# Four transformer blocks on one core: shorter prologues, and the division by the sums on VectorE tile by tile

## The chip, the core and the metric

The kernel runs on one core of a Trainium2 chip. Its engines work from queues of their own: TensorE (PE, with its weight loads as PEld), VectorE (DVE), ScalarE (ACT), GpSimd (POOL) and SyncE (SP, which issues the transfers here). The metric is the device time of one execution in microseconds (us); less is better.

## The reference

The input x is 4 x 1024 x 512 in float32. Four blocks are added to it, each on a layer norm of what the one before left:

```python
x = x + squared_attention(layernorm(x))   # 16 heads of 32; weights (q.k)**2, causal; o / (z + EPS); Wo
x = x + gated_attention(layernorm(x))     # a gate picks one key and one value head per token; causal softmax
x = x + multi_query_attention(layernorm(x))  # one key and value head, biases, causal softmax, output product
x = x + gated_attention(layernorm(x))
```

In each attention, the weights of a query are summed over its keys, the products of weights and values are divided by that sum, and the result goes through an output product or (gated) a plain transposition.

## The kernel before

The program has two acts. The first holds the squared attention, one stage for each of the 4 batch items. The second holds 12 softmax stages: gated, multi-query, gated, 4 items each. A stage has 4 phases of 4 heads. A phase has 20 halves: in each even half PE scores a burst of keys (`keys`, 10 a phase: keys on partitions, up to 512 queries beside), whose exponentials ACT writes to one of 5 slots of `probs`; in 9 of the odd halves PE scores a burst of the next phase's queries (`rows`), of which DVE takes the maxima (L961, L966) that the next phase's exponentials need. Bursts go through three pairs of PSUM banks, two pairs a burst, so that PE can't fill the second pair of a key burst before DVE has read the first pair of the row burst ahead of it. GpSimd masks the diagonal tiles (`keys`, L758) and adds the probabilities up over the key tiles (`add`, L774 to L781), into `added`. PE multiplies probabilities and values (`av`, parts A and B for the first and second chunk of 512 queries, C for the rest of the second) into `y`, and sums `added` over partitions (`sm`); ACT copies the sums to `sums`. DVE inverts them in place, four tiles of 128 columns for each chunk (`inv`, L1068), and GpSimd multiplies the 512 columns of `y` by the inverses (`nrm`, L829). The last chunk of all does both on DVE (`last_nrm`, L1062, L1063).

All else (the next stage's norm, queries, keys, values, gates and the outputs `out` of the stage before) is work that fills PE between the bursts. It goes through two further PSUM banks, cut in pieces, and each bank is free again when ACT or DVE has emptied it: for `kall` and `vall` (all heads' keys and values of a tile, of which the gate picks one) by a multiplication and a reduction on DVE (L945, L949). Python makes one list of events, and each engine runs its own part of that list in its order. `phase` places the fixed events in the halves; `spread` gives each half filling work in proportion to a table of room, which `phase` raises by `INVERTED` in a half with an inverse. Each act begins with a prologue: what its first phase needs, written out ahead of the first half by `plan` and `keys_and_values`. In the first act these are values (`v2`), queries and keys (`q2`, `k2`) and the keys' variances (`ksq` and `kvar`, whose powers GpSimd takes, L821), for two phases.

Of the kernel before, what the change touches and what calls it, by code (L numbers as in the profile page):

```python
# [90 lines left out]
INVERTED = 0.85  # L91

# [27 lines left out]
def keys_and_values(kind, s):  # L120

    if kind == "squared":
        values = [("v2", s, pair, n) for pair in range(2) for n in range(NT // 2)]
        between = values[0:2] + values[4:6]
        return between, values[2:4] + values[6:8] + features(4 * s), features(4 * s + 1)
    queries = [[("q", 4 * s + g, c) for c in range(NC)] for g in range(2)]
    if kind == "gated":
        first = [("gt", s, 1), ("gtt", s, 0), queries[0][0], ("gtt", s, 1), ("gate", s), ("gate_exp", s), queries[0][1], ("gate_value", s)]
        first += [("kall", s, t) for t in range(NT)]
        first.insert(len(first) - 1, ("krep", s, 0))  # L130
        first += [queries[1][0], ("krep", s, 1), ("kt", s, 0), queries[1][1], ("kt", s, 1)]
        return [("gt", s, 0)], first, [("vall", s, t) for t in range(NT)]
    rest = [("vs", s, 0), ("vs", s, 1), queries[1][0], ("vst", s, 0), queries[1][1], ("vst", s, 1)]
    return [("ks", s, 0), queries[0][0]], [("ks", s, 1), queries[0][1]], rest
# [33 lines left out]
def sums_done(kind, ph, c):  # L168

    if kind != "squared":  # L170

        return [(("inv", ph, c, n), min(n + 1, 3 + c)) for n in range(TPC)] + [(("nrm", ph, c), 3 + c)]
    return [(("nrm", ph, c), 2)]


def phase(kinds, ph):
# [34 lines left out]
    for c in range(NC):  # L211
        of = ph - c
        if of < 0:
            continue
        first = SUMS_AT[c] - (4 if final and c == 0 else 0)
        at[first].append(("sm", of, c))
        for event, later in sums_done(kinds[of // NG], of, c):
            at[first + later].append(event)
            if event[0] == "inv":
                room[first + later] += INVERTED  # L220
# [3 lines left out]
def since(event):  # L224

    event = event[1] if event[0] == "more" else event
    if event[0] in ("q", "q2", "k2"):
# [96 lines left out]
def plan(kinds):  # L324
# [7 lines left out]
    else:  # L332
# [5 lines left out]
        events += between + first  # L338
    if soft:
        rows = [("rows", 0, k) for k in range(NRB)]  # L340
        for n in range(max(len(rows), len(rest))):
# [6 lines left out]
    else:  # L348
        events += rest
    for s in range(stages):  # L350
# [33 lines left out]
        else:  # L384
            own = [[("q", 4 * s + g, c) for c in range(NC)] for g in (2, 3)]
            work = [(head[0], 1), (sprinkled(parted(own[0]), head[1]), HALVES - 2), (mixed(parted(outs[:half]), parted(own[1]), kinds), 2 * HALVES - 2)]
        if s == stages - 1:
# [26 lines left out]
class Signals:  # L414


    def __init__(self, nc, ctx):
# [34 lines left out]
        self.inverted = sem("inverted")  # L452
# [117 lines left out]
def act_program(nc, sg, k, psum, m, weights, stages, source, result, dram):  # L570
# [91 lines left out]
    with nc.Block() as block:  # L662
# [61 lines left out]
        def _(pool):  # L724
# [17 lines left out]
            for e in events:  # L742
# [81 lines left out]
                elif u == "nrm" and soft:  # L824
                    _, ph, c = e
                    pool.wait_ge(sg.inverted, place["inv", ph, c, TPC - 1] + 1)
                    wait_free(pool, ("av", ph, "AC"[c]))
                    out = y_of(ph)[:, CHUNK * c:CHUNK * c + CHUNK]
                    pool.tensor_tensor(out, out, m["sums"][:, c], ALU.mult).then_inc(sg.normalized, 1)  # L829
# [8 lines left out]
        def _(act):  # L838
# [19 lines left out]
            for e in events:  # L858
# [57 lines left out]
                elif u == "sm":  # L916
                    _, ph, c = e
                    if ph:
                        act.wait_ge(sg.normalized, place["nrm", ph - 1, c] + 1)
# [3 lines left out]
        def _(dve):  # L923
# [27 lines left out]
            for e in events:  # L951
# [112 lines left out]
                elif u == "inv":  # L1064
                    _, ph, c, n = e
                    wait_free(dve, ("sm", ph, c))
                    some = tile_of(m["sums"][:, c], n)
                    dve.reciprocal(some, some).then_inc(sg.inverted, 1)  # L1068
# [19 lines left out]
        def _(pe):  # L1088
# [55 lines left out]
            for event in events:  # L1144
# [168 lines left out]
                elif u == "out":  # L1313
                    _, s, t = e
                    out = free(e)
                    for g in range(NG):
                        ph = NG * s + g
                        if ("nrm", ph, t // TPC) in place:
                            pe.wait_ge(sg.normalized, place["nrm", ph, t // TPC] + 1)
# [75 lines left out]
```

## Time and profile before

| | us |
|---|---|
| median of 3 runs | 4017.52 (4014.93 to 4022.45) |
| profiled execution, device time | 4020.66 |
| its span, from first to last instruction | 4018.9 |
| PE busy | 3647.1 (91%) |
| GpSimd busy | 2982.7 (74%) |
| DVE busy | 2170.1 (54%) |
| ACT busy | 1624.3 (40%) |

A busy share is an average over stages with different limits. Idle time of an engine counts only where another one waits for it. PE's records overlap and their ends are modelled, so its busy time is read as an occupancy, and its idle time (span less busy) as what waits cost it. The first act ends near 1011 us, the second runs to the end.

### The profile page before, as it was taken

The numbers are of one execution on the slowest core, as the hardware profiler recorded it, in microseconds if no ns is written. First come the engines' busy times: TensorE is split into PE (matmuls) and PEld (weight loads), VectorE is DVE, ScalarE is ACT, GpSimd is POOL, SyncE is SP. The second block draws the span as 40 slices with busy tenths as digits, with TensorE's granted clock in tenths as the row PEclk, the third lists the DMA queues.
The fourth block names the chain that finished last, engine by engine and source line by source line (L and its number), as shares of the span: only waits on it lengthen the run. The fifth ranks groups of instructions, "written<-read, shape, count | busy, mean of one in ns | idle before, by whom it ended". The sixth has DMA issues, their size and how long they took to land.

```text
span 4018.9 us, 66697 instructions
## 1 busy us (share of the span) xinstructions
PE 3647.1 (91%) x25570; PEld 1450.4 (36%) x25570; DVE 2170.1 (54%) x5132; ACT 1624.3 (40%) x2433; POOL 2982.7 (74%) x2207
## 2 busy tenths in 40 slices
PE   8899999997989999999888888888998999999976
PEld 5343534432333333333333333333333333333332
DVE  1222323233556766666666656565665666676663
ACT  1554545554043333434444434343332334343343
POOL 3988788896067767777888877787667677776786
PEclk9999999998999999999999999999999999999997
DMA  2000101020110010100101010010101001010011
GB/s 74 27 6 27 38 16 48 6 70 33 45 33 1 32 32 1 64 1 25 40 13 53 6 48 12 30 35 17 48 1 35 30 1 64 1 54 1 1 43 32
DMA packets 63286, 115.02 MB, mean 29 GB/s; under 512 B 8576, under 2 KB 9088, under 8 KB 62976
## 3 DMA queue, kind: packets, MB, share of 16 engines
q1 hardware_dynamic: 62976, 110.75, 8.5%
q8 instruction: 211, 3.46, 0.4%
q14 instruction: 99, 0.81, 0.1%
HBM read 77.17 MB, written 33.55 MB: 28 GB/s over the span
## 4 chain that ended last, share of the span: by engine, by line
PE 54%; DVE 7%; ACT 6%; issue 4%; POOL 3%; DMA 0%; POOLq 0%; SPq 0%; DVEq 0%; ACTq 0%
PE banks L1181 11%; PE banks L1134 11%; PE banks L1166 9%; PE banks L1228 8%; PE banks L1127 7%; ACT probs_soft L870 5%; PE banks L1163 3%; DVE banks L966 3%; PE banks L1327 3%; DVE maxima_soft L961 2%; POOL added_soft L781 2%; PE banks L1195 1%; DVE rest_soft L1085 1%; DVE maxima_soft L966 1%; PE banks L1325 0%
## 5 line engine op out<-in xcount | busy, mean ns | idle before, releaser
L870 ACT ACTIVATE probs_soft<-banks 128x1024 f32<-128x1024 f32 (+1 forms) x960 | 848.4, 936 | 1195.1 <-PE banks L1166 1171.2
L781 POOL TENSOR_TENSOR added_soft<-added_soft,probs_soft 128x512 f32<-128x512 f32 (+1 forms) x380 | 1153.0, 3034 | 21.3 <-POOL added_soft L774 6.4
L966 DVE CUSTOM_DVE_ANT_0 banks<-banks,mask 128x128 f32<-128x128 f32 (+3 forms) x1536 | 701.3, 528 | 516.5 <-PE banks L1181 516.0
L961 DVE TENSOR_REDUCE maxima_soft<-banks 128x2 f32<-128x1024 f32 x384 | 452.6, 1221 | 367.5 <-PE banks L1181 367.4
L1181 PE MATMUL banks<-k_soft,q_soft 32*128 32x512 f32 (+3 forms) x4608 | 499.7, 525 | 77.6 <-ACT probs_soft L870 77.4
L876 ACT ACTIVATE probs_squared<-banks,key_scale_squared 128x512 f32<-128x512 f32 (+3 forms) x768 | 379.7, 590 | 341.5 <-PE banks L1166 337.1
L1127 PE MATMUL banks<-xnT,wide 128*128 128x512 f32 x1024 | 509.9, 620 | 5.0 <-DVE rest_soft L1085 1.9
L1134 PE MATMUL banks<-wide,xnT 128*128 128x512 f32 x1024 | 497.0, 613 | 1.0 <-ACT q_soft L853 1.0
L1166 PE MATMUL banks<-q_soft,k_soft 32*128 32x512 f32 (+3 forms) x4608 | 476.0, 495 | 0.0
L758 POOL TENSOR_SCALAR_AFFINE_SELECT probs_soft<-probs_soft 128x512 f32<-128x512 f32 x384 | 239.4, 637 | 313.8 <-ACT probs_soft L870 308.3
L1228 PE MATMUL banks<-probs_soft,v_soft 128*32 128x512 f32 (+3 forms) x4608 | 438.3, 499 | 20.2 <-ACT q_soft L855 4.8
L774 POOL TENSOR_TENSOR added_soft<-probs_soft 128x2048 f32<-128x2048 f32 x48 | 216.7, 4514 | 270.9 <-ACT probs_soft L870 270.9
L781 POOL TENSOR_TENSOR added_squared<-added_squared,probs_squared 128x512 f32<-128x512 f32 (+1 forms) x124 | 378.3, 3051 | 4.5 <-POOL added_squared L774 1.4
L1068 DVE RECIPROCAL sums_soft<-sums_soft 128x128 f32<-128x128 f32 x380 | 338.1, 924 | 16.7 <-ACT sums_soft L853 16.6
L1181 PEld LDWEIGHTS banks<-k_soft,q_soft 32*128 32x128 f32 x4608 | 184.1, 186 | 358.5 <-issue 353.4
L1163 PE MATMUL banks<-shift_soft,ones 32*128 32x512 bf16 (+3 forms) x2304 | 197.9, 332 | 88.1 <-DVE maxima_soft L966 57.6
L1134 PEld LDWEIGHTS banks<-wide,xnT 128*128 128x128 f32 x1024 | 175.9, 189 | 262.9 <-issue 251.1
L1127 PEld LDWEIGHTS banks<-xnT,wide 128*128 128x128 f32 x1024 | 178.3, 192 | 254.2 <-issue 236.2
L1228 PEld LDWEIGHTS banks<-probs_soft,v_soft 128*32 128x32 f32 x4608 | 122.3, 110 | 329.7 <-issue 225.1
L1166 PEld LDWEIGHTS banks<-q_soft,k_soft 32*128 32x128 f32 x4608 | 213.2, 187 | 24.4 <-issue 20.9
L966 DVE DVE_READ_ACCUMULATOR2_ANT maxima_soft<- 128x1 f32 x1536 | 220.6, 144 | 0.0
L1163 PEld LDWEIGHTS banks<-shift_soft,ones 32*128 32x128 bf16 x2304 | 62.9, 91 | 417.3 <-issue 390.3
(136 smaller groups left out, 4075.7 us busy)
## 6 DMA issues: line engine op xcount, KB each, us to landing
tiles<-out SPq DMA_DIRECT2D x96, 256.0 KB, 2.7
rest_soft<-out SPq DMA_DIRECT2D x96, 256.0 KB, 2.9
out<-rest_soft SPq DMA_DIRECT2D x96, 256.0 KB, 2.1
tiles<-in_x SPq DMA_DIRECT2D x32, 256.0 KB, 2.7
rest_squared<-in_x SPq DMA_DIRECT2D x32, 256.0 KB, 2.8
out<-rest_squared SPq DMA_DIRECT2D x32, 256.0 KB, 2.0
wide<-in_gated_wqkvT SPq DMA_DIRECT2D x3, 1024.0 KB, 7.6
probs_squared<-in_squared_wk SPq DMA_DIRECT2D x1, 1024.0 KB, 5.5
```

The source lines that it names most:

```text
L781: ins = pool.tensor_tensor(sums, sums, slot(ph, n)[:, :, col:col + width], ALU.add)
L870: ins = act.activation(slot(ph, n)[:, 2 * a:2 * a + 2, 0:width], score_pair(e, a)[:, :, 0:width], ACT.Exp, scale=SCALE)
L876: ins = act.activation(slot(ph, n)[:, i, col:col + cols], score_pair(e, a)[:, x, col:col + cols], ACT.Square, scale=m["key_scale"][:, ph % ...
L961: ins = dve.reduce_max(m["maxima"][:, ph % 2, 2 * a:2 * a + 2, t, p], score_pair(e, a)[:, :, col:col + width], AX_X)
L966: ins = dve.tensor_tensor_reduce(scores, scores, k["mask"][:, CHUNK - width:CHUNK], 1.0, MASKED, ALU.add, ALU.max, m["maxima"][:, ph % 2, ...
L1068: dve.reciprocal(some, some).then_inc(sg.inverted, 1)
L1127: ins = pe.matmul(out, wt[:, kc, cols], m["xnT"][:, kc, CHUNK * c:CHUNK * c + CHUNK], start=(kc == 0), stop=(kc == KC - 1))
L1134: ins = pe.matmul(out, m["xnT"][:, kc, P * t:P * t + P], wt[:, kc, cols], start=(kc == 0), stop=(kc == KC - 1))
L1163: pe.matmul(psum[:, score_bank(e, i), col:col + width], k["ones16"][D * i:D * i + D, :], m["shift"][D * i:D * i + D, ph % 2, c, q0:q0 + wi ...
L1166: ins = pe.matmul(psum[:, score_bank(e, i), col:col + width], k_of(ph)[D * i:D * i + D, P * kb:P * kb + P], m["q"][D * i:D * i + D, ph % N ...
L1181: ins = pe.matmul(psum[:, score_bank(e, i), col:col + P * blocks], m["q"][D * i:D * i + D, ph % NG, P * t:P * t + P], k_of(ph)[D * i:D * i ...
L1228: ins = pe.matmul(out[D * i:D * i + D, q0:q0 + width], left, slot(ph, n)[:, i, col:col + width], start=(x == 0), stop=(x == len(products) ...
```

## The change

Four things are changed. In the first act the prologue keeps half of the values and the features of one phase; the other half and the features of the second phase become filling work of the first phases. In the second act's prologue one query product and two value tiles move behind the first row burst or into the first phase. `INVERTED` goes, so that halves with an inverse get no more filling work than others. And the softmax stages' `nrm` on GpSimd goes: DVE multiplies each tile of 128 columns right behind its inverse, each product with a wait for the inverse ahead of it. `out` then waits for single tiles.

```diff
-INVERTED = 0.85
@@ keys_and_values
+        if s == 0:
+            return [("gt", s, 0)], first + [("krep", s, 1), queries[1][0], ("kt", s, 0), ("kt", s, 1)], \
+                [queries[1][1]] + [("vall", s, t) for t in range(NT)]
         first += [queries[1][0], ("krep", s, 1), ("kt", s, 0), queries[1][1], ("kt", s, 1)]
@@ sums_done
-        return [(("inv", ph, c, n), min(n + 1, 3 + c)) for n in range(TPC)] + [(("nrm", ph, c), 3 + c)]
+        return [(("inv", ph, c, n), min(n + 1, 3 + c)) for n in range(TPC)]
@@ phase
             at[first + later].append(event)
-            if event[0] == "inv":
-                room[first + later] += INVERTED
@@ since
+    if event[0] == "v2" and event[1] == 0 or event[0] in ("q2", "k2") and event[1] < NG:
+        return 0
@@ plan
-        events += between + first
+        values = [e for e in between + first if e[0] == "v2"]
+        events += [e for e in values if e[2] == 0] + [e for e in first if e[0] != "v2"]
+        behind_first = [(in_pieces(rest, kinds), HALVES - 2), (in_pieces([e for e in values if e[2]], kinds), 2 * HALVES + 4)]
     if soft:
         rows = [("rows", 0, k) for k in range(NRB)]
+        behind_first = [(in_pieces(rest[len(rows) - 2:], kinds), 6)]
+        rest = rest[:len(rows) - 2]
...
-    else:
-        events += rest
...
+        if s == 0:
+            work = work[:1] + behind_first + work[1:]
@@ gpsimd
-                elif u == "nrm" and soft:
-                    _, ph, c = e
-                    pool.wait_ge(sg.inverted, place["inv", ph, c, TPC - 1] + 1)
-                    wait_free(pool, ("av", ph, "AC"[c]))
-                    out = y_of(ph)[:, CHUNK * c:CHUNK * c + CHUNK]
-                    pool.tensor_tensor(out, out, m["sums"][:, c], ALU.mult).then_inc(sg.normalized, 1)
@@ scalar, sm
-                        act.wait_ge(sg.normalized, place["nrm", ph - 1, c] + 1)
+                        act.wait_ge(sg.normalized, place[("inv", ph - 1, c, TPC - 1) if soft else ("nrm", ph - 1, c)] + 1)
@@ vector, inv
                     wait_free(dve, ("sm", ph, c))
-                    some = tile_of(m["sums"][:, c], n)
-                    dve.reciprocal(some, some).then_inc(sg.inverted, 1)
+                    wait_free(dve, ("av", ph, "AC"[c]))
+                    some, out = tile_of(m["sums"][:, c], n), tile_of(y_of(ph)[:, CHUNK * c:CHUNK * c + CHUNK], n)
+                    then(dve.reciprocal(some, some))
+                    dve.tensor_tensor(out, out, some, ALU.mult).then_inc(sg.normalized, 1)
@@ tensor, out
-                        if ("nrm", ph, t // TPC) in place:
-                            pe.wait_ge(sg.normalized, place["nrm", ph, t // TPC] + 1)
+                        done = ("inv", ph, t // TPC, t % TPC) if soft else ("nrm", ph, t // TPC)
+                        if done in place:
+                            pe.wait_ge(sg.normalized, place[done] + 1)
```

DVE, in the second multi-query stage, from the end of the last row burst of a phase (L966) to the first row burst behind it, before:

```order
L966 ISA banks,maxima_soft<-banks,mask 128x512
L966 ISA maxima_soft 128x1
L974 TENSOR_REDUCE minus_max_soft<-maxima_soft 128x4x4
L1068 RECIPROCAL sums_soft<-sums_soft 128x128 x4
L966 ISA banks,maxima_soft<-banks,mask 128x128
```

And after:

```order
L964 ISA banks,maxima_soft<-banks,mask 128x512
L964 ISA maxima_soft 128x1
L972 TENSOR_REDUCE minus_max_soft<-maxima_soft 128x4x4
L1067 RECIPROCAL sums_soft<-sums_soft 128x128
L1068 TENSOR_TENSOR y_soft<-y_soft,sums_soft 128x128
L1067 RECIPROCAL sums_soft<-sums_soft 128x128
L1068 TENSOR_TENSOR y_soft<-y_soft,sums_soft 128x128
L1067 RECIPROCAL sums_soft<-sums_soft 128x128
L1068 TENSOR_TENSOR y_soft<-y_soft,sums_soft 128x128
L1067 RECIPROCAL sums_soft<-sums_soft 128x128
L1068 TENSOR_TENSOR y_soft<-y_soft,sums_soft 128x128
L964 ISA banks,maxima_soft<-banks,mask 128x128
```

Between the two row bursts stand four inverses and four products in turn, where four inverses stood.

GpSimd, in the same phase, from the first addition of its second chunk (L774; L778 after) to the mask of the next phase's first key burst, before:

```order
L774 TENSOR_TENSOR added_soft<-probs_soft 128x2048
L781 TENSOR_TENSOR added_soft<-added_soft,probs_soft 128x2048
L758 AFFINE_SELECT probs_soft<-probs_soft 128x4x128
L829 TENSOR_TENSOR y_soft<-y_soft,sums_soft 128x512
L781 TENSOR_TENSOR added_soft<-added_soft,probs_soft 128x2048
L758 AFFINE_SELECT probs_soft<-probs_soft 128x4x128 x2
L781 TENSOR_TENSOR added_soft<-added_soft,probs_soft 128x2048
L758 AFFINE_SELECT probs_soft<-probs_soft 128x4x128
L781 TENSOR_TENSOR added_soft<-added_soft,probs_soft 128x4x384
L781 TENSOR_TENSOR added_soft<-added_soft,probs_soft 128x4x128
L829 TENSOR_TENSOR y_soft<-y_soft,sums_soft 128x512
L758 AFFINE_SELECT probs_soft<-probs_soft 128x4x128
```

And after:

```order
L778 TENSOR_TENSOR added_soft<-probs_soft 128x2048
L785 TENSOR_TENSOR added_soft<-added_soft,probs_soft 128x2048
L762 AFFINE_SELECT probs_soft<-probs_soft 128x4x128
L785 TENSOR_TENSOR added_soft<-added_soft,probs_soft 128x2048
L762 AFFINE_SELECT probs_soft<-probs_soft 128x4x128 x2
L785 TENSOR_TENSOR added_soft<-added_soft,probs_soft 128x2048
L762 AFFINE_SELECT probs_soft<-probs_soft 128x4x128
L785 TENSOR_TENSOR added_soft<-added_soft,probs_soft 128x4x384
L785 TENSOR_TENSOR added_soft<-added_soft,probs_soft 128x4x128
L762 AFFINE_SELECT probs_soft<-probs_soft 128x4x128
```

The two divisions of `y` are gone, and masks and additions stand in the order in which they stood.

PE, from the first act's values (L1288) on, before (L1127 are queries and keys, L1296 variances, L1166 scores of keys):

```order
L1288 MATMUL banks<-wide,xnT 128x256 x64
L1127 MATMUL banks<-xnT,wide 128x512 x16
L1296 MATMUL banks<-head_mean,key_square_squared 128x4 x8
L1127 MATMUL banks<-xnT,wide 128x512 x16
L1296 MATMUL banks<-head_mean,key_square_squared 128x4 x8
L1166 MATMUL banks<-q_squared,k_squared 128x512 x4
L1127 MATMUL banks<-xnT,wide 128x512 x4
L1166 MATMUL banks<-q_squared,k_squared 128x384 x4
```

And after:

```order
L1288 MATMUL banks<-wide,xnT 128x256 x32
L1127 MATMUL banks<-xnT,wide 128x512 x16
L1296 MATMUL banks<-head_mean,key_square_squared 128x4 x8
L1166 MATMUL banks<-q_squared,k_squared 128x512 x4
L1127 MATMUL banks<-xnT,wide 128x512 x6
L1166 MATMUL banks<-q_squared,k_squared 128x384 x4
L1166 MATMUL banks<-q_squared,k_squared 128x128 x4
L1127 MATMUL banks<-xnT,wide 128x512 x6
```

Ahead of the first scores, 32 products of values, 16 of queries and keys and 8 of variances are gone; they follow between the scores.

## Rows read from the trace of the kernel before

**Rows 1.** stretches: us, busy PE, PEld, DVE, ACT, POOL (instructions), PEclk, DMA

```profile
96.00:256.30 160.30, 139.06 (x861) 67.86 (x862) 48.10 (x54) 87.27 (x173) 144.26 (x87) 0.94 0.06 21
...
1598.00:1846.00 248.00, 234.32 (x1729) 88.68 (x1729) 164.82 (x416) 95.01 (x126) 180.30 (x143) 0.99 0.08 27
2057.30:2269.30 212.00, 184.82 (x1609) 69.56 (x1610) 141.86 (x375) 96.49 (x125) 179.48 (x142) 0.98 0.10 31
```

**Rows 2.** PE's waits from 2057.3 to 2269.3 us, multi-query stage

```profile
PE banks L1163 <- DVE maxima_soft L966: 10.2, 15, 1.6
```

**Rows 3.** groups of instructions, whole program: busy us, mean ns, idle before

```profile
L781 POOL TENSOR_TENSOR added_soft<-added_soft,probs_soft 128x512 f32<-128x512 f32 (+1 forms) x380 | 1153.0, 3034 | 21.3 <-POOL added_soft L774 6.4 <-POOL shift_cols_soft L794 0.2 <-POOL added_soft L781 0.2
...
L1068 DVE RECIPROCAL sums_soft<-sums_soft 128x128 f32<-128x128 f32 x380 | 338.1, 924 | 16.7 <-ACT sums_soft L853 16.6
...
L829 POOL TENSOR_TENSOR y_soft<-y_soft,sums_soft 128x512 f32<-128x512 f32 x95 | 121.0, 1274 | 0.0
```

**Rows 4.** the divisions of DVE by line: duration ns min/median/max

```profile
L1063 DVE TENSOR_TENSOR y_soft<-y_soft,sums_soft x4: 291/291/291, 4008.6 to 4012.1; 128x128 f32<-128x128 f32 x4
...
L1076 DVE TENSOR_TENSOR y_squared<-y_squared,sums_squared x31: 691/2323/4984, 140.6 to 968.5; 128x512 f32<-128x512 f32 x31
```

**Rows 5.** GpSimd and DVE at 467 us (start us, us, engine, line)

```profile
467.41 4.51 POOL L781 TENSOR_TENSOR added_squared<-added_squared,probs_squared 128x2048 f32<-128x2048 f32 x1 [0.17 <-POOL added_squared L774]
...
467.50 4.98 DVE L1076 TENSOR_TENSOR y_squared<-y_squared,sums_squared 128x512 f32<-128x512 f32 x1
```

**Rows 6.** GpSimd and DVE at 1189 us

```profile
1189.55 1.27 POOL L781 TENSOR_TENSOR added_soft<-added_soft,probs_soft 128x512 f32<-128x512 f32 x1
1189.60 1.37 DVE L1010 TENSOR_TENSOR gate_soft<-chosen_soft,top_soft 128x128 f32<-128x128 f32 x1
```

**Rows 7.** timeline, end of a phase in the multi-query stage

```profile
2211.96 4.54 POOL L781 TENSOR_TENSOR added_soft<-added_soft,probs_soft 128x2048 f32<-128x2048 f32 x1
...
2213.65 3.38 DVE L1068 RECIPROCAL sums_soft<-sums_soft 128x128 f32<-128x128 f32 x4
...
2217.04 4.79 POOL L781 TENSOR_TENSOR added_soft<-added_soft,probs_soft 128x1536 f32<-128x1536 f32 x2
...
2219.66 0.30 DVE L966 CUSTOM_DVE_ANT_0 banks<-banks,mask 128x128 f32<-128x128 f32 x1 [2.63 <-PE banks L1181]
...
2221.45 0.34 PE L1163 MATMUL banks<-shift_soft,ones 32*128 32x384 bf16 x4 [0.17 <-DVE maxima_soft L966]
```

**Rows 8.** timeline, middle of the same phase

```profile
2196.43 1.75 DVE L1068 RECIPROCAL sums_soft<-sums_soft 128x128 f32<-128x128 f32 x2
...
2197.59 4.52 POOL L781 TENSOR_TENSOR added_soft<-added_soft,probs_soft 128x2048 f32<-128x2048 f32 x1 [0.17 <-POOL added_soft L774]
...
2199.69 2.36 DVE L961 TENSOR_REDUCE maxima_soft<-banks 128x2 f32<-128x1024 f32 x2 [1.51 <-PE banks L1181]
...
2201.06 0.40 PE L1163 MATMUL banks<-shift_soft,ones 32*128 32x512 bf16 x4 [0.15 <-DVE maxima_soft L961]
```

**Rows 9.** timeline, end of a phase in a gated stage

```profile
1530.96 3.38 DVE L1068 RECIPROCAL sums_soft<-sums_soft 128x128 f32<-128x128 f32 x4
...
1534.36 4.77 POOL L781 TENSOR_TENSOR added_soft<-added_soft,probs_soft 128x1536 f32<-128x1536 f32 x2
...
1540.53 1.71 PE L1228 MATMUL banks<-probs_soft,v_soft 128*32 128x512 f32 x16
```

**Rows 10.** timeline of PE, first act: prologue, and a unit of values later

```profile
79.03 13.98 PE L1127 MATMUL banks<-xnT,wide 128*128 128x512 f32 x32
...
163.60 3.72 PE L1288 MATMUL banks<-wide,xnT 128*128 128x256 f32 x16
```

**Rows 11.** timeline of PE, end of the second act's prologue

```profile
1097.75 3.70 PE L1134 MATMUL banks<-wide,xnT 128*128 128x512 f32 x8
```

**Rows 12.** timeline, last phase of all

```profile
3980.66 5.01 DVE L1068 RECIPROCAL sums_soft<-sums_soft 128x128 f32<-128x128 f32 x6 [1.05 <-ACT sums_soft L853]
...
3993.36 3.71 PE L1325 MATMUL banks<-ident,y_soft 128*128 128x128 f32 x16 [7.91 <-POOL y_soft L829]
```

More of the change, by code:

```diff
@@ L451, in __init__ @@
         self.last_normalized = sem("last_normalized")
-        self.inverted = sem("inverted")
         self.normalized = sem("normalized")
```

## The prediction

> **What bounds the kernel now.** I read the table of engines first, then stretches, the waits in them, the groups of instructions, and at last the timeline around the inverses. PE is busy 91% of the span and the other engines 40 to 74%, so PE's order of work is the bound, and a gain has to come out of PE's idle time. The stretches tell where that is [rows 1]: the first phases after the prologue leave PE 160.30 − 139.06 = 21.2 us idle, a gated stage 248.00 − 234.32 = 13.7 us (3.4 a phase) and a multi-query stage 212.00 − 184.82 = 27.2 us (6.8 a phase), at granted clocks of 0.94, 0.99 and 0.98, so nearly all at the 2.4 GHz level. In the multi-query stage GpSimd is busy 85% (179.48) and DVE 67% (141.86); of PE's waits there one is for DVE's maxima: 15 times, 10.2 us in all, 1.6 at the longest [rows 2]. DVE is off the bound on average, but once or more a phase PE stands at a pair of banks that DVE has yet to read. What the change adds to DVE is therefore priced at those places and not as a share of busy time.
>
> **The division by the sums.** GpSimd loses 95 products of 512 columns, 121.0 us; DVE gets 380 of 128 columns, one behind each of 380 inverses of 924 ns [rows 3]. Alone, a product of this shape takes DVE 291 ns (the last chunk's four, when GpSimd has nothing to do) [rows 4]. So 380 × 0.29 = 110 us of DVE work replace 121.0 of GpSimd's, if nothing else acts.
>
> Something else acts. The same division in the first act, 512 columns, takes 691 ns at the least, 2323 in the middle and 4984 at most [rows 4]. Its longest starts 0.09 us behind a GpSimd addition of 4.51 us and ends at 472.48, which is 0.56 us behind the addition's end at 471.92 [rows 5]. A 128x128 product of the second act starts 0.05 us behind an addition of 1.27 us, takes 1.37 instead of some 0.29, and ends 0.15 behind the addition [rows 6]. So a DVE product with both inputs in SBUF is held until the GpSimd operation under way is done. The inverses, one input each, aren't held: four take 3.38 us beside an addition of 4.54 [rows 7], and the mean of all is 924 ns.
>
> A rule of the Trainium skill speaks to this ("SBUF — State Buffer", section Who interferes with whom): a VectorE instruction with two SBUF inputs contends with a GpSimd instruction that reads SBUF, over a port pair that whoever issues first locks, and the other is fully blocked. The 4984 ns of rows 5 and the 1370 ns of rows 6 agree with it. By that rule the change sends 380 instructions into the lock; without it they would be 0.29 us each.
>
> Each held product also holds up the inverse behind it. I walk the three places that recur, putting each product at the end of the addition that it meets.
>
> End of a multi-query phase [rows 7]. The inverses start at 2213.65. The first ends at 2214.5; its product is held to the end of the addition, 2211.96 + 4.54 = 2216.5, or 2216.1 if GpSimd is 0.35 earlier for the missing division (my allowance). The second inverse ends 0.9 later, inside the next two additions (4.79 us together), and since one follows the other without a gap its product is out at the end of the first (1.27 and 3.45 by the order's shapes, the longer ahead), near 2220.3. The last two pairs are out near 2221.7 and 2222.9. DVE is free at about 2223.0, where it was at 2213.65 + 3.38 = 2217.03: 6.0 us later. It waited 2.63 us for PE there and read the next row burst from 2219.66; it now reads it from 2223.0, 3.3 us late, and the key burst whose second pair PE filled at 2221.45, 0.17 behind DVE's maxima, follows as late. PE pays +3.3 us.
>
> Middle of the phase [rows 8]. Of two inverses from 2196.43 the first product is out by 2197.6, the second meets the addition of 2197.59 to 2202.11 and is out at 2202.3. DVE turned to the row burst at 2199.69 with 1.51 us of slack; it is 2.6 late, and PE, 0.15 behind it at 2201.06, loses about +2.4. The two first inverses of a chunk stand in a half of their own, and I allow 0.5 for theirs: 6.2 a phase where there is little filling work.
>
> End of a gated phase [rows 9]. The inverses end at 1534.34; with the products, two of them held by the 4.77 us of additions, at about 1539.5, 5.2 later. DVE's reading of key products for the gate comes behind it and frees the bank of `av` part C (1540.53) 2 to 3 us later; PE has filling work for part of that. I take 2 us, and 1.5 for the middle: 3.5 a phase.
>
> About 19 phases are light (multi-query ones and the last ones) and 27 full: 19 × 6.2 + 27 × 3.5 = 118 + 95 = 213 us. PE's idle time a phase is already 6.8 and 3.4 us [rows 1], as large as these stalls, and a stall that falls before another wait shortens it. I take a third off: +142. Ends: 40, if lateness mostly falls into the idle time that there is (with the gains below that is 4025), and 260, if each stall adds up and the halves with more products pay too. Below nothing it can't go: nothing that PE waits for gets earlier by more than GpSimd's relief. That relief is small: `out` already stands a phase behind its division, and the adds start 0.35 us to 1.3 earlier in a queue of GpSimd that seldom ends last; −2 (0 to −20).
>
> **The first act's prologue.** Four units of values of 3.72 us and the second phase's features, 13.98 [rows 10], go behind the first scores: 14.9 + 14.0 = 28.9 us of PE work. It isn't saved; it fills. The three phases from 96 us have 21.2 us idle [rows 1], of which some 3.4 a phase are left in a well-filled stage, so about 11 can be filled; and some work ran while the clock was lower (0.94 against 0.99 later), worth 0.05 × 160 = 8 at most, half taken. −15, from −5 (the moved values come with waits for DVE's copies, and for GpSimd's powers of the variances) to −27 (all but the 1.9 that doesn't fit).
>
> **The second act's prologue.** Two units of value tiles, 3.70 each [rows 11], and a query product move behind the first row burst. PE then waits there for maxima and exponentials that start earlier: −3, from −5 to +1.
>
> **Room without `INVERTED`.** The filling work of a stage stays as it was; the last halves of a phase get less and the early ones more. The early halves have part of the 3.4 and 6.8 us idle, the late ones get shorter just where DVE is now late (counted above). Over 48 phases I take 0.2 each: −10, from −25 to +10.
>
> **The end.** PE's 7.91 us wait for GpSimd's last division goes, but the six inverses ahead of it, from 3980.66 [rows 12], now carry products beside GpSimd's last additions: 0, from −8 to +3.
>
> Sum: 142 − 2 − 15 − 3 − 10 = +112. On the profiled execution's 4020.66 us (span 4018.9) that is 4133; the median of the runs is 3.1 lower, so 4130. The case's own range, from the stalls' two ends with the other terms, is 4025 to 4240.
>
> **Rivals.**
> *The cover holds, and it is faster.* The products slip between GpSimd's operations, or DVE's lateness at the next row burst stays under the slack that it has (2.63 and 1.51 us in rows 7 and 8); it decides as long as a cluster of inverses ends less than about 2 us later than before. For it: DVE is idle 46% of the span, and L781's additions fill only 1153 of the second act's some 3000 us [rows 3]. Against: the inverses stand in the order just where additions follow each other without a gap. Then −15 − 3 − 10 − 5 = −33: 3985.
>
> The Trainium skill speaks for this rival ("GPSIMD Engine Reference", section 4.1 Engine selection): elementwise work belongs on VectorE, GpSimd being about twice as slow with two inputs. Rows 3 and 4 agree, 1274 ns against 4 × 291, but these four ran while GpSimd was idle.
>
> *DVE becomes the bound.* L781's additions fill 1153 of the second act's some 3000 us; a product that starts at any moment would be held 0.38 × 3034 / 2 = 0.6 us, and behind long additions, as in the walks, more: I take 1.1. 380 × 1.1 + 110 = 530 us more on DVE, and where PE follows DVE burst by burst three quarters of it, 400, show: 4390. For it: rows 2 and 7, where PE starts 0.17 us behind DVE. Against: DVE would still have 2170 + 530 = 2700 of 4100 us.
>
> *The gains and the stalls cancel.* Half of the lower end of the stalls, 30, against 30: within some 8 us of 4017, if only the ends of multi-query phases are hit.
>
> **How the numbers follow.** Slower by held products 0.68; the cover holds 0.20; DVE the bound 0.06; cancelling 0.06, of which 0.04 lie within 0.2% (8 us, about what a measurement of this kernel can tell from no change) and 0.01 to each side. Faster 0.21, same 0.04, slower 0.75. The likeliest case gives 4130. The range takes in the rival on the other side, 3985, and reaches to the upper end of the likeliest case, 4240; DVE as the bound is left out.
>
> **What would show it.** The group of `y_soft` products on DVE with a mean of 1.2 to 1.6 us (0.29 proves the holding wrong); DVE's busy time near 2600 to 2700; more and longer waits of PE for `maxima_soft` in the multi-query stages, 3 us where 1.6 was the longest; the GpSimd group of 95 divisions gone, and its additions no longer than 3034 ns. The first act should end some 15 us earlier whatever the second does. If the products are held and PE's waits for maxima don't grow, the cover was larger than rows 7 and 8 say; if the first act isn't shorter, the moved work met waits for DVE.

## The result and the profile after

The changed kernel takes 4317.05 us (4315.86 to 4318.33, four runs) where the kernel before took 4018.23 beside it: a ratio of 1.0743, 95% interval 1.0724 to 1.0762. The forecast was slower by 112 us, with 4240 as the upper end; it is 299 us, and outside the range. Direction and place were as forecast; the size was not.

Stretches of the changed kernel, in the columns of [rows 1]: the three phases that were 96 to 256.3 us, the gated stage, the multi-query stage, and then what lies ahead of the second act's first burst of keys and what lies behind it. PEclk is the share of TensorE's clock that was granted: 1.00 is 2.4 GHz, 0.50 is 1.2.

```profile
69.30:239.30 170.00, 164.66 (x965) 84.48 (x964) 49.89 (x62) 90.22 (x176) 148.10 (x89) 0.98 0.07 19
1633.00:1908.20 275.20, 243.66 (x1729) 89.64 (x1730) 200.03 (x448) 95.01 (x125) 171.08 (x135) 0.96 0.07 24
2162.90:2413.10 250.20, 197.74 (x1609) 73.55 (x1609) 182.14 (x408) 95.92 (x124) 170.45 (x134) 0.92 0.08 26
0.00:1088.60 1088.60, 999.21 (x5475) 454.87 (x5476) 332.56 (x457) 489.43 (x956) 811.11 (x507) 0.97 0.11 36
1088.60:4315.70 3227.10, 2746.01 (x20096) 1011.77 (x20096) 2287.73 (x5056) 1135.36 (x1478) 2065.78 (x1605) 0.95 0.07 23
```

The kernel before, its second act from the first burst of keys on:

```profile
1105.70:4018.90 2913.20, 2643.62 (x20080) 990.69 (x20080) 1833.27 (x4672) 1135.87 (x1478) 2172.28 (x1700) 0.98 0.08 26
```

The second act's first burst of keys comes 17.1 us earlier (1088.6, was 1105.7), and of the 21.2 us idle of the first act's first phases 170.00 − 164.66 = 5.3 are left. Not all of the 17.1 is the first act's. PE's first product of the second act, after and before:

```profile
1005.85 1.92 PE L1140 MATMUL banks<-xnT,g_wg 128*32 128x512 f32 x16 [3.97 <-PEq L1331]
...
1015.89 2.64 PE L1140 MATMUL banks<-xnT,g_wg 128*32 128x512 f32 x16 [3.99 <-PEq L1330]
```

So the first act gains 10.0 us, and the other 7.1 are the second act's shorter prologue, whose moved work is done later. From the first burst of keys on (called the second act from here) the kernel is 313.9 us longer. PE's idle time in it went from 2913.20 − 2643.62 = 269.6 to 3227.10 − 2746.01 = 481.1, +211.5; the other 102.4 us are PE's own busy time, for as many matmuls (20096, 20080), at a granted clock of 0.95 where it was 0.98.

Groups of the changed kernel, against [rows 3]:

```profile
L785 POOL TENSOR_TENSOR added_soft<-added_soft,probs_soft 128x512 f32<-128x512 f32 (+1 forms) x380 | 1152.9, 3034 | 20.9 <-POOL added_soft L778 5.9 <-ACT probs_soft L868 0.2 <-POOL added_soft L785 0.2
...
L1068 DVE TENSOR_TENSOR y_soft<-y_soft,sums_soft 128x128 f32<-128x128 f32 x380 | 447.3, 1177 | 13.0
...
L1067 DVE RECIPROCAL sums_soft<-sums_soft 128x128 f32<-128x128 f32 x380 | 357.7, 941 | 12.3 <-ACT sums_soft L851 12.2
```

A product takes 1177 ns in the mean in place of the 291 of [rows 4]: 447.3 − 380 × 0.291 = 337 us of holding. It is spread unevenly: half of the products take 442 ns or less, the longest 4616. The mean of GpSimd's additions is the same as before, 3034 ns: what waits is DVE. PE's largest waits in the whole run:

```profile
PE banks L1163 <- DVE maxima_soft L959: 105.7, 69, 5.5
PE banks L1163 <- DVE maxima_soft L964: 97.4, 57, 5.3
PE banks L1228 <- DVE picking_soft L943: 57.7, 21, 3.9
PE banks L1181 <- ACT probs_soft L868: 49.7, 107, 1.3
```

Before they read, for the same four:

```profile
PE banks L1181 <- ACT probs_soft L870: 77.4, 187, 1.4
PE banks L1163 <- DVE maxima_soft L966: 57.6, 70, 1.9
...
PE banks L1163 <- DVE maxima_soft L961: 22.4, 42, 1.4
...
PE banks L1228 <- DVE picking_soft L945: 4.7, 9, 0.5
```

Waits for maxima went from 80.0 to 203.1 us, those of `av` (L1228) for a bank in which DVE has yet to read the gate's keys and values (`picking_soft`) from 4.7 to 57.7, while those for ACT's exponentials fell by only 27.7.

The timeline of the changed kernel, middle of the phase that [rows 8] show:

```profile
2330.41 4.52 POOL L785 TENSOR_TENSOR added_soft<-added_soft,probs_soft 128x2048 f32<-128x2048 f32 x1 [0.17 <-POOL added_soft L778]
2331.42 3.67 DVE L1068 TENSOR_TENSOR y_soft<-y_soft,sums_soft 128x128 f32<-128x128 f32 x1
...
2335.01 2.34 DVE L959 TENSOR_REDUCE maxima_soft<-banks 128x2 f32<-128x1024 f32 x2
...
2336.36 0.40 PE L1163 MATMUL banks<-shift_soft,ones 32*128 32x512 bf16 x4 [3.01 <-DVE maxima_soft L959]
```

The second product starts 1.01 us into the addition and ends 0.16 behind it; DVE turns to the row burst at once, and PE, which was 0.15 behind DVE here, waits 3.01. The end of the same phase, where [rows 7] had four inverses in 3.38 us and PE 0.17 behind the maxima:

```profile
2346.98 4.51 POOL L785 TENSOR_TENSOR added_soft<-added_soft,probs_soft 128x2048 f32<-128x2048 f32 x1
...
2348.95 0.94 DVE L1067 RECIPROCAL sums_soft<-sums_soft 128x128 f32<-128x128 f32 x1
2349.93 1.71 DVE L1068 TENSOR_TENSOR y_soft<-y_soft,sums_soft 128x128 f32<-128x128 f32 x1
...
2352.10 4.79 POOL L785 TENSOR_TENSOR added_soft<-added_soft,probs_soft 128x1536 f32<-128x1536 f32 x2
2352.53 3.17 DVE L1068 TENSOR_TENSOR y_soft<-y_soft,sums_soft 128x128 f32<-128x128 f32 x1
...
2356.59 0.44 DVE L1068 TENSOR_TENSOR y_soft<-y_soft,sums_soft 128x128 f32<-128x128 f32 x1
...
2357.93 0.29 DVE L1068 TENSOR_TENSOR y_soft<-y_soft,sums_soft 128x128 f32<-128x128 f32 x1
2358.14 0.29 DVE L964 CUSTOM_DVE_ANT_0 banks<-banks,mask 128x128 f32<-128x128 f32 x1
...
2359.91 0.51 PE L1163 MATMUL banks<-shift_soft,ones 32*128 32x384 bf16 x4 [4.34 <-DVE maxima_soft L964]
...
2360.18 1.52 PE L1166 MATMUL banks<-q_soft,k_soft 32*128 32x384 f32 x8
```

Four inverses and products fill 2348.95 to 2358.22, 9.3 us. And the last row shows what came after the wait: eight matmuls of 384 columns in 1.52 us. Eighteen microseconds earlier they took

```profile
2342.50 0.81 PE L1166 MATMUL banks<-q_soft,k_soft 32*128 32x384 f32 x8
```

The granted clock in between (columns of [rows 1]):

```profile
2338.00:2344.00 6.00, 6.00 (x68) 1.93 (x64) 4.01 (x6) 2.49 (x4) 4.26 (x2) 1.00 0.00 0
2352.00:2358.90 6.90, 3.34 (x34) 0.98 (x32) 6.80 (x11) 1.55 (x2) 6.53 (x9) 1.00 0.00 1
2359.00:2365.70 6.70, 5.79 (x48) 2.54 (x48) 2.98 (x13) 1.94 (x2) 3.57 (x3) 0.50 0.00 0
2366.00:2372.00 6.00, 5.40 (x46) 2.49 (x49) 5.09 (x18) 2.26 (x4) 2.62 (x3) 1.00 0.00 0
```

PE is busy for 3.34 of the 6.90 us in which it waits for DVE, and then runs 6.7 us at 1.2 GHz (0.50). So this wait costs twice. Added up from the trace's records of the granted clock, the second act spends 335 us at 1.2 GHz, where it was 111; half of the 224 us between them, 112, is an estimate of what that costs, close to the 102 that PE's busy time grew.

### The profile page after: what moved, and what is told of

Read it like the earlier page. It is cut to its first block and busy times, and to the rows that moved or that the text cites. A ratio compares the mean times of both kernels' runs of the same rounds, so it can differ in the third digit from the quotient of the medians.

```text
span 4315.7 us, 67265 instructions
## 1 busy us (share of the span) xinstructions
PE 3745.2 (87%) x25570; PEld 1466.6 (34%) x25570; DVE 2620.3 (61%) x5512; ACT 1624.8 (38%) x2433; POOL 2876.9 (67%) x2112
## 5 line engine op out<-in xcount | busy, mean ns | idle before, releaser
L785 POOL TENSOR_TENSOR added_soft<-added_soft,probs_soft 128x512 f32<-128x512 f32 (+1 forms) x380 | 1152.9, 3034 | 20.9 <-POOL added_soft L778 5.9
L1181 PE MATMUL banks<-k_soft,q_soft 32*128 32x512 f32 (+3 forms) x4608 | 504.5, 529 | 51.5 <-ACT probs_soft L868 49.7
L1228 PE MATMUL banks<-probs_soft,v_soft 128*32 128x512 f32 (+3 forms) x4608 | 473.4, 533 | 66.5 <-DVE picking_soft L943 57.7
L1127 PE MATMUL banks<-xnT,wide 128*128 128x512 f32 x1024 | 514.6, 623 | 6.6 <-DVE rest_soft L1085 2.4
L1134 PE MATMUL banks<-wide,xnT 128*128 128x512 f32 x1024 | 508.4, 622 | 13.0 <-DVE picking_soft L943 12.8
L1166 PE MATMUL banks<-q_soft,k_soft 32*128 32x512 f32 (+3 forms) x4608 | 506.5, 523 | 0.0
L1068 DVE TENSOR_TENSOR y_soft<-y_soft,sums_soft 128x128 f32<-128x128 f32 x380 | 447.3, 1177 | 13.0
L778 POOL TENSOR_TENSOR added_soft<-probs_soft 128x2048 f32<-128x2048 f32 x48 | 216.7, 4514 | 340.5 <-ACT probs_soft L868 276.7
L1067 DVE RECIPROCAL sums_soft<-sums_soft 128x128 f32<-128x128 f32 x380 | 357.7, 941 | 12.3 <-ACT sums_soft L851 12.2
L1127 PEld LDWEIGHTS banks<-xnT,wide 128*128 128x128 f32 x1024 | 177.8, 192 | 260.2 <-issue 240.6
L1228 PEld LDWEIGHTS banks<-probs_soft,v_soft 128*32 128x32 f32 x4608 | 127.6, 115 | 406.6 <-issue 264.8
L1166 PEld LDWEIGHTS banks<-q_soft,k_soft 32*128 32x128 f32 x4608 | 225.8, 198 | 29.0 <-issue 24.3
```

Of the source, the lines that this page charges most:

```text
L785: ins = pool.tensor_tensor(sums, sums, slot(ph, n)[:, :, col:col + width], ALU.add)
L1067: then(dve.reciprocal(some, some))
L1068: dve.tensor_tensor(out, out, some, ALU.mult).then_inc(sg.normalized, 1)
L1127: ins = pe.matmul(out, wt[:, kc, cols], m["xnT"][:, kc, CHUNK * c:CHUNK * c + CHUNK], start=(kc == 0), stop=(kc == KC - 1))
L1134: ins = pe.matmul(out, m["xnT"][:, kc, P * t:P * t + P], wt[:, kc, cols], start=(kc == 0), stop=(kc == KC - 1))
L1166: ins = pe.matmul(psum[:, score_bank(e, i), col:col + width], k_of(ph)[D * i:D * i + D, P * kb:P * kb + P], m["q"][D * i:D * i + D, ph % N ...
```

## The experiments

Two theories stood against the held products (H in the expectations) at first: that the early halves, which take the filling work once INVERTED is gone, cost the time (R), and that a product on DVE costs by its work and waits, whatever GpSimd does (W).

**Products back on GpSimd.** The edit puts `nrm` back and takes the products out of `inv`; all else as changed:

```diff
-        return [(("inv", ph, c, n), min(n + 1, 3 + c)) for n in range(TPC)]
+        return [(("inv", ph, c, n), min(n + 1, 3 + c)) for n in range(TPC)] + [(("nrm", ph, c), 3 + c)]
...
-                    then(dve.reciprocal(some, some))
-                    dve.tensor_tensor(out, out, some, ALU.mult).then_inc(sg.normalized, 1)
+                    dve.reciprocal(some, some).then_inc(sg.inverted, 1)
```

> The changed kernel with the softmax stages' products back on GpSimd (512 columns at a time) and all else as changed. Theory H (products that are held behind GpSimd's additions make DVE late, PE waits for DVE, and its granted clock falls): the whole loss goes and the shorter prologues stay, 3985 to 4005 us, DVE busy near 2170. Rival R (taking INVERTED out put too much filling work into the early halves, and that is what costs): still over 4050 us.

3959.99 us, ratio to the kernel before 0.9849 (0.9834 to 0.9864): 357 us less than the changed kernel, and 25 under the lower end of what H gave. The products are the loss; R falls, and the other edits gain 61 us.

**Products alone**, on the kernel before (the same edit the other way round).

> The kernel before with only the products moved to DVE, tile by tile behind each inverse; prologues and INVERTED as before. Theory H: nearly the whole second act's loss of 314 us shows, 4300 to 4350 us, products with a mean near 1.2 us. Rival R: with the room behind inverses kept, the loss is under 230 us, below 4250.

4298.06 us, 1.0688 (1.067 to 1.0706): +277, 2 us under what H gave and far over R's 4250. Its products have a mean of 1252 ns. The two stages of [rows 1] in this run, where the room behind inverses is as before:

```profile
1635.80:1902.40 266.60, 237.59 (x1729) 90.57 (x1729) 207.56 (x448) 95.18 (x126) 171.06 (x135) 0.97 0.08 25
2147.30:2393.00 245.70, 194.12 (x1609) 72.23 (x1609) 181.22 (x407) 96.46 (x124) 169.88 (x133) 0.94 0.08 27
```

and PE's waits for ACT's exponentials in the whole run, 77.4 us before:

```profile
PE banks L1176 <- ACT probs_soft L863: 73.6, 180, 1.4
```

**Additions that only write.** The edit for one addition; the first ones of each chunk are replaced likewise:

```diff
+            def written(cells):
+                then(pool.memset(cells, 1.0))
+                then(pool.memset(cells, 1.0))
+                return pool.memset(cells[:, 0:HG // 2], 1.0)
...
-                        ins = pool.tensor_tensor(sums, sums, slot(ph, n)[:, :, col:col + width], ALU.add)
+                        ins = written(sums) if soft else pool.tensor_tensor(sums, sums, slot(ph, n)[:, :, col:col + width], ALU.add)
```

> The changed kernel in which GpSimd's additions of the softmax stages are replaced by fills of the same tiles (two and a half fills for each addition, so about as long: 4.6 us where an addition takes 4.5); the sums of the weights are left out by that. GpSimd then writes SBUF and reads none of it. Theory H: the products take 0.29 us, PE's waits for DVE's maxima fall from 203 us to about 80, and the time is 3980 to 4040 us. Rival W (the products are DVE work with waits of their own, and DVE is late by its amount of work, whatever GpSimd does): products stay near 1.2 us, the time over 4250.

3967.51 us, 0.9867 (0.9852 to 0.9881), 12 us under the range of H; the waits for maxima are 44.4 + 31.0 = 75.4 us. The fills keep GpSimd busy 615.8 + 615.8 + 331.3 = 1563 us, as long as the additions they replace (1152.9 + 216.7 + 164.8 = 1534). The end of a multi-query phase in this run, products now at L1073:

```profile
2147.33 1.80 POOL L748 MEMSET added_soft<- 128x2048 f32 x1
...
2148.17 0.29 DVE L1073 TENSOR_TENSOR y_soft<-y_soft,sums_soft 128x128 f32<-128x128 f32 x1
...
2149.36 0.29 DVE L1073 TENSOR_TENSOR y_soft<-y_soft,sums_soft 128x128 f32<-128x128 f32 x1
...
2153.83 0.34 PE L1168 MATMUL banks<-shift_soft,ones 32*128 32x384 bf16 x4 [0.17 <-DVE maxima_soft L969]
```

and the group of all products:

```profile
L1073 DVE TENSOR_TENSOR y_soft<-y_soft,sums_soft 128x128 f32<-128x128 f32 x380 | 120.2, 316 | 13.0
```

A product beside a GpSimd operation that reads no SBUF takes 0.29 us, and PE is back at 0.17 behind the maxima. W falls. The rule of the Trainium skill named in the prediction ("SBUF — State Buffer", Who interferes with whom) says the same: it is GpSimd's reading that contends, not its writing. Not held, the products are still no gain here: 3968 against 3960 on GpSimd, with intervals that touch, and with fills that run 29 us longer than the additions.

**The four products behind the last inverse**, in a row.

```diff
                     then(dve.reciprocal(some, some))
-                    dve.tensor_tensor(out, out, some, ALU.mult).then_inc(sg.normalized, 1)
+                    if n == TPC - 1:
+                        for n in range(TPC):
+                            some, out = tile_of(m["sums"][:, c], n), tile_of(y_of(ph)[:, CHUNK * c:CHUNK * c + CHUNK], n)
+                            dve.tensor_tensor(out, out, some, ALU.mult).then_inc(sg.normalized, 1)
...
-                        done = ("inv", ph, t // TPC, t % TPC) if soft else ("nrm", ph, t // TPC)
+                        done = ("inv", ph, t // TPC, TPC - 1) if soft else ("nrm", ph, t // TPC)
```

> The changed kernel with the four products of a chunk behind its fourth inverse, one after the other, and `out` waiting for all four. Theory H: one hold a chunk, at most one addition, and the other three products slip through behind it: the sum of the products falls from 447 us to 200 to 300, the time to 4130 to 4220 us. Rival W: same work of DVE, same time within 20 us of 4317. Rival H2 (each product is held anew, by the next addition, even when it is ready): the sum of the products rises over 600 us and the time over 4350.

4163.85 us, 1.0355 (1.0339 to 1.037); products 281.1 us, mean 799 ns. The holding fell from 337 to 281 − 111 = 170 us, and the loss against products on GpSimd from 357 to 204. H's figures hold, W's and H2's don't. The order of DVE's own instructions decides how long it is held.

**Each inverse a second time**, an edit of the run with products on GpSimd.

```diff
-                    dve.reciprocal(some, some).then_inc(sg.inverted, 1)
+                    then(dve.reciprocal(some, some))
+                    dve.reciprocal(some, some).then_inc(sg.inverted, 1)
```

> The changed kernel with its products on GpSimd (3960 us), and each inverse taken a second time in place, so that the sums themselves and not their inverses go into the products: DVE gets 380 operations of 0.94 us more, which nothing holds, where the held products took 1.18. Theory H (what costs is that DVE comes late to the next row burst, by whatever makes it late, and PE's granted clock then falls after its waits): 4130 to 4260 us, PE's waits for maxima over 140 us, and the time at the lower clock in the second act over 200 us where it was 89. Rival W (work that is not held is absorbed by DVE's idle time, only the hold itself costs): under 4000 us.

4120.73 us, 1.0251 (1.0236 to 1.0266): 161 more than the run with products on GpSimd, by 380 further inverses, 362 us of DVE work that nothing holds. That is 9 us under what H gave, and its 186 us at 1.2 GHz are under the 200; this experiment's W (such work is absorbed) is far off. PE's waits for maxima:

```profile
PE banks L1169 <- DVE maxima_soft L971: 71.4, 56, 3.5
...
PE banks L1169 <- DVE maxima_soft L966: 53.7, 58, 3.0
```

125 us where the expectation had over 140. So lateness of DVE behind the inverses costs by itself; holding is one way to make it late, and here a dearer one: 362 us of unheld work cost 161, 447 us of products with their holding 357. That it is dearer because it comes in lumps of up to 4 us wasn't tested.

**The gains apart**, each alone on the kernel before:

```diff
+    if event[0] == "v2" and event[1] == 0 or event[0] in ("q2", "k2") and event[1] < NG:
+        return 0
```

(with the first act's lines of `plan` from the change)

> The kernel before with only the first act's prologue shortened. By the trace of the changed kernel, whose first act ends 17 us earlier: 4001 to 4007 us where the kernel before has about 4021 on the same chip. Rival (what is moved only changes places, and the first act's end is set elsewhere): within 4 us of before.

4005.29 us, 0.9963 (0.9949 to 0.9977): −15. The expectation took all of the 17 us for the first act's. Over all the runs, the second act's first product starts at 999 to 1011 us with this prologue (nine profiles) and at 1016 to 1019 without it (four).

```diff
+        behind_first = [(in_pieces(rest[len(rows) - 2:], kinds), 6)]
+        rest = rest[:len(rows) - 2]
```

(with the lines of `keys_and_values` from the change)

> The kernel before with only the second act's prologue shortened. By the prediction, 3 us less; if a large part of the 61 us that the change gains without its products comes from here, 10 to 25 us less.

4024.23 us, 1.0009 (1.0000 to 1.0019): no gain, and 4 us lost at the edge of what can be told.

```diff
-INVERTED = 0.85
...
-            if event[0] == "inv":
-                room[first + later] += INVERTED
```

> The kernel before with only INVERTED taken out, the products on GpSimd. The change without its products gains 61 us, of which the first act has 18; if the rest is due to INVERTED, this one is 35 to 45 us faster than before. By the prediction, 10 us. Rival: no difference, the rest comes from the second prologue.

3965.74 us, 0.9866 (0.9851 to 0.988): −54, more than any of the figures expected. The second act, in the columns of [rows 1]:

```profile
1107.40:3962.80 2855.40, 2630.57 (x20083) 980.73 (x20080) 1836.92 (x4672) 1135.15 (x1478) 2170.18 (x1700) 0.99 0.08 27
```

Idle time is 224.8 where it was 269.6, and PE's busy time is 13 less. The waits for exponentials, 77.4 before, are

```profile
PE banks L1177 <- ACT probs_soft L866: 58.0, 123, 1.3
```

**INVERTED back in the changed kernel.**

```diff
+INVERTED = 0.85
...
+            if event[0] == "inv":
+                room[first + later] += INVERTED
```

> The changed kernel with INVERTED put back. The products alone cost 277 us on the kernel before, and the prologues together with INVERTED's removal 19 us more, though without the products they give 61. Theory I (the extra filling work behind inverses is PE's cover where DVE is late: its removal gains 54 us without held products and costs some 30 with them): 4275 to 4300 us, faster than the changed kernel's 4317. Rival A (the edits add up: INVERTED's removal gains here too): 4340 to 4380 us.

4284.36 us, 1.0659 (1.0641 to 1.0677): 33 us faster than the changed kernel, in the range of theory I and well under A's. The same edit that gains 54 us where products run on GpSimd costs 33 where they are held. From this run to the changed kernel the waits of `av` for `picking_soft` go from 29.5 to 57.7 us and those for maxima from 178.3 to 203.1, while those for exponentials fall from 71.7 to 49.7. That fits I's reason, that the filling work behind inverses covers DVE's lateness; no run tests the reason apart. The single effects add up to the whole: 4018 − 15 + 4 + 277 + 33 = 4317.

**What gained by itself, together**: the first prologue and no INVERTED, products on GpSimd and the second prologue as before.

> The kernel before with the first act's shorter prologue and without INVERTED, products on GpSimd, second prologue as before: the two parts that gained by themselves, -15 and -54 us. If they add up 3949 to 3956 us, below the 3960 of the version that has the second prologue too; rival (no difference from that one): 3957 to 3965.

3953.11 us, 0.9838 (0.9823 to 0.9852), the lowest of all runs, in the range for gains that add up, and 7 below the one with the second prologue too, with intervals that overlap.

**Less room than nothing.**

```diff
-INVERTED = 0.85
+INVERTED = -0.4
```

> As the version with the first act's shorter prologue and products on GpSimd, but INVERTED at -0.4 in place of 0.85 or nothing, so that halves with an inverse get less filling work than others. If PE's idle time in early halves is still what filling work is worth: 3930 to 3950 us. If the even table is where it ends: 3955 to 3990.

4008.82 us, 0.9977 (0.9967 to 0.9986): worse than without INVERTED by 56, and over both ranges that were expected. The waits for exponentials are longer than without it (69.6 and 18.6 us, at L1185 and L1167, where they were 58.7 and 8.6), those for maxima about the same; why is open. Of the three values tried, 0 is the best.

The second act in these runs; idle is its length less PE's busy time, the time at 1.2 GHz is added up from the records of the granted clock:

| | time | one product, ns | PE idle | PE busy | at 1.2 GHz |
|---|---|---|---|---|---|
| before | 4018 | | 269.6 | 2643.6 | 111 |
| changed | 4317 | 1177 | 481.1 | 2746.0 | 335 |
| products alone | 4298 | 1252 | 470.4 | 2718.5 | 308 |
| products last | 4164 | 799 | 371.2 | 2700.7 | 232 |
| inverses twice | 4121 | | 347.3 | 2687.7 | 186 |
| additions only write | 3968 | 316 | 236.6 | 2641.5 | 80 |
| products on GpSimd | 3960 | | 227.0 | 2640.4 | 89 |

With as many matmuls in each (20080 to 20096), more idle time goes with more time at 1.2 GHz and more busy time: from the last row to that of the changed kernel, 254 us more idle time go with 246 more at the lower clock and 106 more of busy time.

## Why the prediction was wrong

**Right: the holding.** A mean of 1.2 to 1.6 us was forecast for a product, and 1177 ns came, just under it; DVE's 2620 us busy lie in the forecast 2600 to 2700. PE's longest wait for maxima in the multi-query stage is 4.5 us, where 3 was forecast. That it is GpSimd's additions that hold them is shown by the fills.

**Right: the walks, before the discount.** The four pairs at the end of the phase were to take from 2213.65 to 2223.0, 9.35 us, and took 9.3; PE was to lose 3.3 there and 2.4 in the middle, and lost 4.34 − 0.17 = 4.2 and 3.01 − 0.15 = 2.9. A multi-query stage has 250.20 − 197.74 = 52.5 us idle where it had 27.2, +6.3 a phase (6.2 forecast); a gated one 275.20 − 243.66 = 31.5 where it had 13.7, +4.5 (3.5 forecast), its end of phase like this:

```profile
1638.50 0.68 DVE L943 TENSOR_TENSOR picking_soft<-banks,gate_soft 128x512 f32<-128x512 f32 x1
...
1639.24 3.13 PE L1228 MATMUL banks<-probs_soft,v_soft 128*32 128x512 f32 x16 [3.35 <-DVE picking_soft L943]
```

PE waits 3.35 us for the bank where 2 were taken. The changed kernel also has INVERTED's removal in these figures. With products alone the same stages have 245.70 − 194.12 = 51.6 and 266.60 − 237.59 = 29.0 us idle, +6.1 and +3.8 a phase. Over the act the walks gave 213 us of stalls, and idle time rose by 470.4 − 269.6 = 200.8 with products alone. Part of that closeness is luck: by stage the rise is 2.9 to 6.1 a phase, and the sum counts 46 of 48 phases.

**The first step that failed: "I take a third off: +142".** The argument was that a stall falling before another wait shortens it. It hardly did. With products alone the waits for ACT's exponentials fell from 77.4 to 73.6 us; most of the 27.7 by which they fell in the changed kernel goes with INVERTED (58.0 in the run that only takes it out). Idle time rose by 200.8 us where 142 − 2 = 140 were forecast: 61 of the 187 us missed (299 less 112).

**The second: a term that the sum did not have.** It priced stalls as idle time alone and took PE's clock as 0.98 to 0.99 throughout. With products alone, PE's busy time rose by 2718.5 − 2643.6 = 75 us with the time at 1.2 GHz going from 111 to 308; in the changed kernel it rose by 102, with 335. [Rows 1] held the hint, in the first act's 0.94 where PE had 21.2 us idle, and the prediction used it for a gain there and not for a loss here. That the clock takes its share follows from equal matmuls in more time at 0.50; no run kept PE busy in its waits, so the two costs of a stall were not separated by an experiment.

**The third: "−10" for INVERTED.** Its removal costs 33 us with held products and gains 54 without. The prediction counted the early halves' idle time, and said that the late halves get shorter just where DVE is late, but took this as counted in the walks, which kept the filling work where it was. Here the term was 43 us too low. The small terms: the first prologue −15 by itself, as forecast (10 us of it show in the changed kernel's first act), the second +4 (−3). So the products' 277 for 140, INVERTED's 33 for −10 and the second prologue's 4 for −3 make up the 187: 137 + 43 + 7. Of the 137, 61 are idle time and 75 PE's longer busy time.

**A slip in the sum.** With the other terms, the stalls' ends of 40 and 260 give 4028 and 4248, not 4025 and 4240; 4317 lies above both.

**The rivals.** The cover that "holds as long as a cluster of inverses ends less than about 2 us later" met clusters that ended 5.9 us later than 3.38: its condition was not met. DVE as the bound would have had 4390, which is nearer to 4317 than the likeliest case's 4130. It took 1.1 us of holding for a product, where 337 us over 380 are 0.89, and three quarters of DVE's further work as loss, where DVE's busy time rose by 2620.3 − 2170.1 = 450 us and two thirds of it, 299, show. As a mechanism it fits less: DVE still idles for 3227 − 2288 = 939 us of the act. For an elementwise product the Trainium skill ("GPSIMD Engine Reference", Engine selection) names VectorE, GpSimd being about twice as slow with two inputs. For one product that holds: 512 columns take DVE 691 ns at the least [rows 4] and GpSimd 1274. The prediction's own pair, 4 × 291 = 1164 against 1274, is a factor of only 1.1, so cutting the product in four had used up most of the gain before any holding. For the kernel, following the preference beside GpSimd's additions lost 357 us, and gained nothing beside fills.

## What to carry to other kernels

Before work is moved between DVE and GpSimd, ask what the other engine is reading while it runs: a DVE product with two SBUF inputs waits here for the end of the GpSimd operation under way, if that reads SBUF, and a chain of inverse and product can meet the next one again. Price a new stall of PE twice, as idle time and as the work at the lower clock that followed it here, and take no discount for other waits unless the trace names the one that shrinks. And test the edits of a combined change apart: here two of the four are worth 66 us by themselves (3953 against 4020), which the products hid.

## What was not expected

GpSimd lost nothing by the products: its additions have a mean of 3034 ns before and after, so the two engines don't share the delay. Filling work behind an inverse has a value of either sign, −54 or +33 us by one constant, depending on whether DVE's products are held there. And a longer inverse chain that nothing holds, 362 us more of an engine that was 54% busy, already cost 161 us.
